# Perceiver block on one core: cross attention in 64-row halves, a reordered end of the history stage, and a convolution by quarters of the heads on VectorE

## The reference

```python
scores = einsum('hqd,hkd->hqk', q, k) * HD ** -0.5
scores = where(mask, 0, scores)
scores = conv3x3(scores, kern[h])          # padding 1
scores = where(mask, -1e30, scores)
x = x + (softmax(scores) @ v) @ proj_W + proj_b
```

## Time and profile before

| | us |
|---|---|
| three runs: median (lowest to highest) | 1029.82 (1022.39 to 1030.22) |
| the profiled execution | 1024.7 |
| its span, from first to last instruction | 1022.9 |
| PE / PEld / DVE / ACT / POOL busy | 856.8 / 668.7 / 636.3 / 542.2 / 128.7 |
| mean granted clock of PE, as a share of 2.4 GHz | 0.888 |

### The profile page before, as it was taken

The page is one execution under the profiler, slowest core; times in us unless marked ns, Lnnn a source line. Parts: engine busy times, 40 slices in busy tenths (PEclk is TensorE's granted clock), DMA queues, the critical chain, the costliest instruction groups (busy, mean ns, idle before and its releaser), DMA issues. The chain is left out here.

```text
span 1022.9 us, 19628 instructions
## 1 busy us (share of the span) xinstructions
PE 856.8 (84%) x7644; PEld 668.7 (65%) x7644; DVE 636.3 (62%) x1132; ACT 542.2 (53%) x1078; POOL 128.7 (13%) x135
## 2 busy tenths in 40 slices
PE   3999999999999998560275857999999999998756
PEld 3988878878788786340144833777777777776544
DVE  3555557767676677779714469677787877721141
ACT  2777777777777777330210001666666666685010
POOL 1232212222222221035000000000000000000010
PEclk9999999999999999885565975999999999999566
DMA  3456535555356551470059095588988987351000
GB/s 113 130 141 191 157 114 145 137 161 140 125 154 164 137 143 57 76 309 0 0 70 150 1 210 144 110 175 142 197 181 136 200 184 138 91 169 40 1 0 6
DMA packets 83139, 126.28 MB, mean 123 GB/s; under 512 B 10755, under 2 KB 73476, under 8 KB 82246
## 3 DMA queue, kind: packets, MB, share of 16 engines
q1 hardware_dynamic: 83046, 125.01, 51.0%
HBM read 85.46 MB, written 39.52 MB: 122 GB/s over the span
## 5 line engine op out<-in xcount | busy, mean ns | idle before, releaser
L1698 DVE TENSOR_REDUCE unit_max<-bank 128x2 f32<-128x896 f32 x224 | 232.5, 1086 | 64.5 <-PE bank L896 64.2
L1222 ACT ACTIVATE prob<-bank 128x512 f32<-128x512 f32 x392 | 205.8, 598 | 82.5 <-PE bank L919 79.4
L919 PE MATMUL bank<-q_stack,k_stack 112*128 112x256 f32 x784 | 129.3, 301 | 0.7 <-ACT q_stack L1215 0.5
L619 PE MATMUL bank<-hc_high,w_high 128*128 128x256 f32 x392 | 117.6, 300 | 8.6 <-POOL hc_low L1276 8.4
L919 PEld LDWEIGHTS bank<-q_stack,k_stack 112*128 112x128 f32 x784 | 102.3, 190 | 31.4 <-ACT prob L1222 17.6
L1395 DVE SCALAR_TENSOR_TENSOR normed<-bank,b_centered,rstd_wide 128x256 f32<-128x256 f32 x196 | 85.5, 478 | 47.6 <-ACT rstd_wide L1090 47.5
L935 PE MATMUL bank<-prob,vals 128*32 128x128 f32 x3136 | 113.4, 278 | 0.0
L619 PE MATMUL bank<-hc_high,w_low 128*128 128x256 f32 x392 | 112.9, 288 | 0.0
L619 PE MATMUL bank<-hc_low,w_high 128*128 128x256 f32 x392 | 112.7, 287 | 0.0
L896 PE MATMUL bank<-k_stack,q_max 49*128 49x448 f32 x448 | 95.8, 484 | 12.5 <-DVE unit_max L1698 11.1
L1083 ACT ACTIVATE square<-bank,b_centered 128x256 f32<-128x256 f32 x196 | 82.0, 472 | 29.1 <-PE bank L619 29.1
(11 more groups left out here) (304 smaller groups left out, 1285.6 us busy)
## 6 DMA issues: line engine op xcount, KB each, us to landing
k_stack<-k_scratch SPq DMA_DIRECT2D x336, 112.0 KB, 5.1
vals<-v_scratch SPq DMA_DIRECT2D x8, 1666.0 KB, 10.4
v_scratch<-vst SPq DMA_DIRECT2D x12, 1088.0 KB, 9.5
hc_raw<-in_ctx_t SPq DMA_DIRECT2D x49, 256.0 KB, 3.0
k_scratch<-k_high SPq DMA_DIRECT2D x49, 256.0 KB, 3.3
k_scratch<-k_low SPq DMA_DIRECT2D x49, 256.0 KB, 3.5
w_ffn<-in_l SPq DMA_DIRECT2D x4, 1920.0 KB, 14.1
w_l<-in_l SPq DMA_DIRECT2D x6, 603.0 KB, 5.4
```

The lines of the kernel that those rows point to most:

```text
L619: last = nc.tensor.matmul(out_ap, lhs, rhs, start=(n == 0), stop=(n == len(pairs) - 1))
L919: last = nc.tensor.matmul(bank[:, at, t * 2 * T:(t + 1) * 2 * T], k_stack[s % 2][0:STACK, k * P:(k + 1) * P], q_stack[0:STACK, s, :], star ...
L1222: A(prob[:, e % NPB, :, :], bank[:, at, :].rearrange("p (u t) -> p u t", u=2), ACT.Exp).then_inc(c_exp, 1)
L1698: V.tensor_reduce(unit_max[:, s % 2, u, :], bank[:, at:at + 2, 0:MU], AX_X, ALU.max, negate=True).then_inc(c_red, 1)
```

## The change

Three parts.

1. **Cross attention.** Unit of work is now UT = 4 tiles of 128 keys (UK = 512 keys; EU = 25 units a pair of heads, the last of two tiles). `scores` does one matmul for each head and tile: keys of 49 rows as weights (rows 0 to 48 or 64 to 112), 128 query columns streamed, the two heads into two banks. `q_stack` has 128 columns a pair and no zeros, and is one copy on DVE in place of two multiplies; the ones row exists at rows 32 and 96. A maxima unit has 512 keys. `exponentials` reads two banks, 1024 columns. DVE reduces the maxima of the first pair of heads 1024 columns at a time, of the other pairs 512 at a time (two instructions a unit), from a ring of three banks that are freed singly. A step has STEP = 2 units: a maxima unit, the scores of two units, a maxima unit, then `weigh` of the two before. `NPB` is 6 buffers of 1024 columns in place of 12 of 512. As many DMAs for a pair of heads as before; `fill` writes two rows of ones.

2. **End of the history stage.** The hidden layers of pairs 22 and 23 use banks 2 and 3, free by then, and no longer wait for `hide_act` of the pair before; `keys_full`, `values_turn` and `values_copy` of the last chunk go ahead of the last pair; the exponentials of group 5 and the weighted sums of group 5 go ahead of, or round, the last logit; the sum over groups is made in the stage, `cc_wide` into a buffer of the stage, before `history_done`; the bias rows of the kernel network are loaded early on their own (`rows_kg`).

3. **Convolution.** DVE does all 16 heads, four at a time (QH = 4): nine taps, one minimum with `cap` (in place of multiply and add), one maximum, and then the next quarter. The copies of the transposed probabilities stand between quarters. POOL does nothing here.

```diff
-            for tap in TAPS:
...
-                for h in range(DVE_HEADS):
...
-            link(V.tensor_tensor(mine, mine, wide(keep), ALU.mult))
-            link(V.tensor_tensor(mine, mine, wide(hide), ALU.add))
-            done(V.tensor_reduce(s_max[:, 0:DVE_HEADS], mine, AX_X, ALU.max, negate=True), "s_max")
-            pool_s.wait(dve, "conv")
-            done(V.tensor_reduce(s_max[:, DVE_HEADS:H], conv[:, DVE_HEADS:H, :], AX_X, ALU.max, negate=True), "s_max_rest")
+            def conv_quarter(b):
+                heads_of = range(QH * b, QH * b + QH)
+                for tap in TAPS:
...
+                        if tap == TAPS[0]:
+                            ins = V.tensor_scalar(conv[:, h, :], src, kern[:, h, tap:tap + 1], None, ALU.mult)
+                        else:
+                            dve.wait_ge(dve_own, own[0] - QH + 1)
+                            ins = V.scalar_tensor_tensor(out=conv[:, h, :], in0=src, scalar=kern[:, h, tap:tap + 1],
+                                                         in1=conv[:, h, :], op0=ALU.mult, op1=ALU.add)
...
+                link(V.tensor_tensor(mine, mine, cap[:, :].unsqueeze(1).broadcast_to([P, QH, T]), ALU.min))
+                done(V.tensor_reduce(s_max[:, QH * b:QH * b + QH], mine, AX_X, ALU.max, negate=True), f"s_max{b}")
...
+            conv_quarter(0)
+            for b in range(1, 4):
+                conv_quarter(b)
+                prob_turned(b - 1)
+            prob_turned(3)
```

```diff
         def w1_bank(i):
-            return {NP - 2: 2, NP - 1: 3}.get(i, 5)
+            return {NP - 3: 2, NP - 2: 3}.get(i, 5)
...
-                if part_of == 0:
+                if part_of == 0 and i < NP - 3:
                     wait_at(pe, h_hid, i)
+                if part_of == 0 and NP - 3 <= i < NP - 1:
+                    pe.wait_ge(h_nm, CT * (NCH - 1))
+                if part_of == 0 and i == NP - 1:
+                    pe.wait_ge(h_hid, NP - 3)
...
             def scores(e):
...
-                for t in range(2):
-                    k = 2 * u + t
-                    last = nc.tensor.matmul(bank[:, at, t * 2 * T:(t + 1) * 2 * T],
-                                            k_stack[s % 2][0:STACK, k * P:(k + 1) * P], q_stack[0:STACK, s, :],
-                                            start=True, stop=True)
+                for t, k in enumerate(unit_tiles(u)):
+                    for hh in range(2):
+                        last = nc.tensor.matmul(bank[:, at + hh, t * T:(t + 1) * T],
+                                                k_stack[s % 2][head_rows[hh], k * P:(k + 1) * P],
+                                                q_stack[head_rows[hh], s, :], start=True, stop=True)
...
-            for exps, turns, groups in step_plan():
+            for exps, turns in step_plan():
+                ahead = [m for m in range(exps[0] + EU + LEAD, exps[-1] + EU + LEAD + 1) if m < EXPS]
+                for m in ahead[0:1]:
+                    maximum(m)
                 for e in exps:
                     scores(e)
+                for m in ahead[1:]:
+                    maximum(m)
...
             def reduce_unit(m):
...
+                if s == 0:
+                    V.tensor_reduce(unit_max[:, 0, u, :], bank[:, at[0]:at[0] + 2, 0:width], AX_X, ALU.max,
+                                    negate=True).then_inc(c_red, 2)
+                else:
+                    for hh in range(2):
+                        V.tensor_reduce(unit_max[:, s % 2, u, hh:hh + 1], bank[:, at[hh], 0:width], AX_X, ALU.max,
+                                        negate=True).then_inc(c_red, 1)
```

More of the change, by code:

```diff
@@ L123, in free, with max_banks, max_freed, unit_tiles @@
         return n - len(self.banks) + 1
+def max_banks(m):
+    ring = FIRST_BANKS if m < EU else MAX_BANKS
+    return [ring[(2 * m + hh) % len(ring)] for hh in range(2)]
+def max_freed(m):
+    return 2 * m + 2 - len(FIRST_BANKS if m < EU else MAX_BANKS)
+def unit_tiles(u):
+    return range(UT * u, min(UT * u + UT, TILES))
 def step_plan():
-    half = UNITS // 2
-    steps, placed, turned = [], half + LEAD, 1
+    steps, placed, turned = [], EU + LEAD, 1
     for j in range(-(-EXPS // STEP)):
@@ L133, in step_plan @@
         turns = []
-        if turned < NG and placed >= half * (turned + 1):
+        if turned < NG and placed >= EU * (turned + 1):
             turns.append(turned)
             turned += 1
-        due = min(half * NG, half + LEAD + STEP * (j + 1) * half // EU)
-        steps.append((exps, turns, range(placed, due)))
-        placed = max(placed, due)
+        steps.append((exps, turns))
+        placed = min(EXPS, placed + len(exps))
     return steps
@@ L905, in turn_maxima @@
                 for hh in range(2):
-                    last = nc.tensor.matmul(bank[MAX_ROW:MAX_ROW + 32, at, hh * T:(hh + 1) * T],
-                                            neg_max[:, hh, :].bitcast(F32), ident, start=True, stop=True)
+                    row = 64 * hh + MAX_ROW
+                    last = nc.tensor.matmul(bank[row:row + 32, at, 0:T], neg_max[:, hh, :].bitcast(F32), ident,
+                                            start=True, stop=True)
                 last.then_inc(c_sc, 1)
@@ L1155, in _ @@
             feature_pair(NCH + 3)
+            keys_full(NCH - 1)
             hide_act(NP - 2)
-            keys_full(NCH - 1)
+            values_copy(NCH - 1)
+            weights(STEADY)
             hide_act(NP - 1)
-            for group in range(STEADY, NGR):
-                weights(group)
-            values_copy(NCH - 1)
+            weights(STEADY + 1)
+            weights(STEADY + 2)
+            dve_s.wait(act, "g_shift")
+            act_s.done(A(g_w[:, :], g_w[:, :], ACT.Exp), "g_w")
             pe_s.wait(act, "xn1_t")
@@ L1425, in mask_rows @@
                 link(V.tensor_scalar(keep[:, :], masked[:, :], -1.0, 1.0, ALU.mult, ALU.add))
-                done(V.tensor_scalar(hide[:, :], masked[:, :], NEG, None, ALU.mult), "mask")
+                link(V.tensor_scalar(masked[:, :], masked[:, :], NEG, None, ALU.mult))
+                done(V.scalar_tensor_tensor(out=cap[:, :], in0=keep[:, :], scalar=-MIN_START, in1=masked[:, :],
+                                            op0=ALU.mult, op1=ALU.add), "mask")
             def spread_x(name):
@@ L1484, in _ @@
             dve.wait_ge(pe_s.sem, 1)
-            done(V.memset(g_one[:, :], 0.0), "history_done")
+            done(V.memset(gone[:, :], 0.0), "history_done")
             def layer_norm(n, src=None):
@@ L1705, in reduce_unit @@
                                     ALU.min).then_inc(c_hm, 1)
-            for s in range(NG):
-                for u in range(UNITS):
-                    reduce_unit(s, u)
+            for m in range(EXPS):
+                reduce_unit(m)
             dve.wait_ge(c_ot, 1)
```

256 lines of the change are left out of this document (111 added, 145 removed).

## The result

The changed kernel takes 991.0 us (median of 988.97, 991.02 and 997.56) against 1029.9: ratio 0.9654, 95% interval 0.9577 to 0.9731. It is faster by 3.5%; 5.8% were forecast. A fourth execution took 1022.0 us at a mean granted clock of 0.846 (the others 0.875 to 0.882) and is left out as a slow one. The profiled execution took 988.97 us (span 987.2), 35.7 less than before.

| stretch | before | after | change | forecast |
|---|---|---|---|---|
| start to first tap | 451.7 | 442.2 | -9.5 | -8 |
| first tap to reciprocal | 65.4 | 55.1 | -10.3 | -15 |
| reciprocal to first maxima | 84.9 | 88.6 | +3.7 | 0 |
| first pair's maxima | 33.6 | 33.1 | -0.5 | -1 |
| first turn to last weighing | 299.9 | 283.4 | -16.5 | -31 |

The account below looks back on a forecast made before the run. PE's order of work bounds the steady attention, VectorE the first maxima and convolution, a chain the history end. From 1024.7: -31 - 1 - 15 - 8 = -55, 969.7, forecast 970; range 952 to 982, with A and B 945 to 1010.

Parts of the forecast that it names:

- rivals A and B: Attention: A, VectorE bounds, step 2.92, time 986, chance 0.16; B, loads wait for the stream before, time 1005, chance 0.07.
- The history end: End of the history stage: fewer waits and an earlier `cc_wide` save 8 us (bounds -4.5 and -9).
- just hidden: History end: the stores, 10.3 us after issue, land near 431, against `cc_wide` at 430.5; if they do not move, -4.5.
- The convolution: First tap to reciprocal: VectorE alone at full rate, four heads behind the last maximum; 50.4 replaces 65.4, -15 us.
- a wait for shifted rows held to be covered: Convolution, first quarter: rows shifted up needed 7.4 us after its start, ready with 1.9 us to spare, costing nothing.
- a quarter of the product 1.71: Convolution's end: only a quarter of the product of probabilities and values, 1.71 us, stands behind the last copy; 5.4 in all.
- The attention: Steady cross attention: eight-tile steps on PE take 269 us with VectorE's waits instead of 300, -31 us.
- The steady step: Cross attention: start 0.21, maxima 0.46, eight tiles of scores 0.92, weighing 1.01, together 2.60 us.
- waits of 12 us: Cross attention: maxima groups' waits for VectorE, the remainder between 288 by prices and the trace's 300, added again to 257.
- rival C: Scores: a tile's halves take turns or a 128-column matmul costs a 256-column one, 0.23 a tile; time 1060, chance 0.15.
- the sum of seven equal pairs and a short one: Cross attention: seven pairs of heads of 32.9 us and a last one of 26.7 without maxima make 257.

Follow-up runs that it names:

- hist_only: The kernel before with the reordered end of the history stage alone: 1019.7 us, ratio 0.9922 to before.
- prod_quarters: The kernel after with each quarter's eight products of probabilities and values behind the next quarter's transposes: median 986.5 us (974.7 to 991.1).
- warm_conv: `prod_quarters` plus seven unused fp32 matmuls behind each convolution quarter but the last, to keep PE busy: profiled run 986.9 us, other three 1003 to 1025.
- conv_only: The kernel before with the new convolution alone (quarters, VectorE alone, one minimum with a cap): 1019.8 us, ratio 0.9914 to before.
- half_reduced: The kernel after with VectorE's reductions reading only 256 of a unit's 512 columns from the second pair of heads on: fastest 974.0 us, others 996 to 1015.
- one_head: The kernel after without the scores of each pair's second head from the second pair of heads on: 1041.5 to 1126.6 us.
- after_again: The kernel after, unchanged, measured once more: 988.1 us (984.9 to 996.7), ratio 0.9596.
- warm_first: The kernel after with one more unused maxima matmul of 512 columns per unit during the first pair's maxima: 1006 to 1042 us.

## Why the prediction was right and wrong

**Direction** was right in all three parts, and so was the mechanism but for one term of the convolution; 19 of 55 us did not come. The time, 991, lies above the forecast's own range (952 to 982) and inside the wider one (945 to 1010), which was drawn with rivals A and B.

**The history end** (-8): -9.5. The stores left VectorE a wait of 0.46 us, as "just hidden" had it; in `hist_only` they left 2.26, so the close fit is in part luck.

**The convolution** (-15): VectorE's part right, 45.5 us to the end of the last row maximum against 45.0, of which 0.9 was a wait for shifted rows held to be covered (0.67 of it for the rows shifted down, which the sum did not look at); 44.4 in the later runs. That GpSimd's silence gives VectorE its full rate from the first instruction is what the Trainium skill says ("SBUF — State Buffer", Who interferes with whom), and the 0.346 us from first to last agrees. The failed step is "a quarter of the product 1.71": PE's program makes all transposes first and then all 32 products, 6.84 us. I read the quarters of the diff into a loop that it does not touch. From the last row maximum to the reciprocal it took 9.6 us, not 5.4. `prod_quarters` confirms the term: with 16 products behind, 3.4 us of it come back.

**The middle** (nothing forecast): 3.7 us given back, by the clock, as `warm_conv` shows. I had costed work and not asked what a stage ahead leaves in the granted clock of the next.

**The attention** (-31): -16.5. The steady step was right. Forecast were 2.60 and waits of 12 us over some 90 steps, together 2.74; measured 2.73, of which PE's own is 2.57. Undisturbed pairs are 34.4 on average, 34.6 forecast. That the waits come out so close is partly luck: the 12 us were a remainder, and some 4 of them were no waits, as said below. Eight tiles and two maxima units take 0.11 + 1.01 + 0.44 = 1.56 us free of VectorE: rival B (0.36 us a step more) and rival C (0.92 more) fall. By the rule of the Trainium skill ("TensorE: Matmul & The Clock Gate", Part 3, The mechanism) loads overlap matmuls of another row group, as these alternating halves are, and here the trace agrees: a tile's two loads and two matmuls in some 0.12 us. Rival A named the right bound, VectorE, and came out near the right time (986), but by a step of 2.92 that does not exist.

The failed step is the sum of seven equal pairs and a short one. The 14.5 us missing are three terms that it put at nothing or too low. The first pair took 4.2 more (the clock is at 0.50 for 15 us behind the first turn, 7 before); this is not the new attention's doing alone, since it was 12 and 15 us in `hist_only` and `conv_only` with the old one, and 15 to 43 in the other profiles. The six pairs that follow took 6.0 more (pauses of PE, its stops for VectorE and the drops of its clock). The last pair took 4.3 more (31.0 against 26.7): its steps take 2.24 us (880.20 to 898.77, less a pause of 0.7) where the sum has 2.14, and at its start PE waits four times for ScalarE, 0.23 to 0.36 us each. That last one hid in my own check: the formula gave 28.1 for today's last pair, which took 31.9, and I booked the difference as waits of the maxima. What sets the clock back, and what makes PE pause, stays open.

```profile
619.00:634.00 15.00, 13.99 (x138) 10.75 (x136) 9.18 (x15) 7.64 (x9) 0.00 (x0) 0.50 0.27 48
```

```profile
635.60:643.00 7.40, 6.67 (x46) 4.85 (x44) 1.31 (x3) 4.71 (x8) 0.00 (x0) 0.51 0.00 0
```

These are the first microseconds behind the first turn, after and before.

## What to carry to other kernels

Check a price list stage by stage against the old trace, not only in the sum: a remainder of 12 us put under one name was two things. Before a stage's work is counted as overlapped, read the other engine's loop in the code, since a change that makes quarters on one engine does not make them on its consumer. And where two stages follow each other on PE, carry its granted clock as a quantity of its own: here it decided 4 us between two untouched stretches, and two runs of the kernel after that lie 33 us apart differ in it (0.882 and 0.846).

## What the runs showed of the hardware

- The granted clock of PE falls from 1.00 to 0.50 inside a full stretch, within 4 us behind a short stop: behind a pause of 1.65 us (785.3 in `half_reduced`), but also behind a wait of 0.81 us for VectorE (664.9 in after, 675.3 in `one_head`). It does not fall behind each (a pause of 1.75 us at 784.9 in after; two of three such waits in `after_again`). Then it stays at 0.50 for 3.4 to 109 us with PE busy throughout. What ends it no run shows.
- Runs of the kernels with the new attention spread more: 29 of before took 1022.4 to 1033.2 us, ten of after 984.9 to 1022.0, and of the kernels with more or less work per step 974 to 1015 (`half_reduced`), 1006 to 1042 (`warm_first`) and 1042 to 1127 (`one_head`).
- PE pauses for 0.7 to 2.8 us with nothing to wait for, 1.1 to 2.3 us behind the start of a 16 KB instruction packet in 23 of 24 cases. With the attention's key and value transfers left out no such pause came in the steady part of the one profile taken (DMA share 0.01, against 0.85 in after from 660 to 860 us).
